# A two-layer pairwise-product network on one core: layer 1 in three rounded passes throughout, five of eight banks to ScalarE in every second tile, GpSimd's program without a loop

## What is computed

```python
for W in filters:                       # x0: 512 x 32 x 32
    z = jnp.einsum('bhd,bmd->bhmd', x0, prev)
    z = z.reshape(b, h * m, d)
    cur = jnp.einsum('bpd,pn->bnd', z, W[0])
    cur = jax.nn.relu(cur)              # 128 maps
    prev = cur
    outs.append(cur)
result = jnp.concatenate(outs, axis=1)
z = jnp.sum(result, axis=-1)            # 512 x 256
...
h = jnp.concatenate([z, dense_ctx], axis=1)
h = jnp.maximum(h @ W_top1 + b_top1, 0.0)
h = jnp.maximum(h @ W_top2 + b_top2, 0.0)
y = h @ W_top3
```

## Time and profile before

| | us |
|---|---|
| median of 3 runs | 882.83 |
| lowest and highest | 880.86, 882.96 |
| profiled execution, its own time | 881.15 |
| its span (first to last instruction) | 879.3 |
| TensorE busy | 854.6 (97%) |
| VectorE busy | 790.5 (90%) |
| ScalarE busy | 681.6 (78%) |
| GpSimd busy | 750.1 (85%) |

### The profile page before, as it was taken

The page is one execution under the profiler, slowest core; times in us unless marked ns, Lnnn a source line. Parts: engine busy times, 40 slices in busy tenths (PEclk is TensorE's granted clock), DMA queues, the critical chain, the costliest instruction groups (busy, mean ns, idle before and its releaser), DMA issues.

```text
span 879.3 us, 18096 instructions
## 1 busy us (share of the span) xinstructions
PE 854.6 (97%) x3581; PEld 669.4 (76%) x3581; DVE 790.5 (90%) x2392; ACT 681.6 (78%) x2230; POOL 750.1 (85%) x834
## 2 busy tenths in 40 slices
PE   2899999999999999999999999999999999999998
PEld 1578777778777777877777787777778777778884
DVE  2689999999999999999999999989999999999984
ACT  2577877888787788888778888777887877888883
POOL 6179989999988999999999999998999989987781
DMA  6786677766667676666777666776766676763430
GB/s 179 205 190 132 157 178 162 181 155 139 126 158 170 163 180 151 136 130 158 173 164 176 142 137 134 164 174 164 167 139 131 144 172 157 182 161 76 88 72 1
DMA packets 55481, 131.16 MB, mean 149 GB/s; under 512 B 8101, under 2 KB 19333, under 8 KB 55462
## 3 DMA queue, kind: packets, MB, share of 16 engines
q0 software_dynamic: 22240, 68.17, 42.8%
q1 hardware_dynamic: 31538, 59.99, 21.2%
q10 hardware_dynamic: 1683, 2.80, 1.0%
HBM read 60.67 MB, written 4.20 MB: 74 GB/s over the span
## 4 chain that ended last, share of the span: by engine, by line
PE 92%; DMA 3%; DVE 2%; SPq 1%; ACT 1%; issue 1%; POOL 0%; DVEq 0%; ACTq 0%
PE t_act L738 13%; PE t_act L740 13%; PE t_act L739 13%; PE t_dve L738 13%; PE t_dve L740 13%; PE t_dve L739 13%; PE acc L706 6%; PE acc L711 5%; DMA x_shift<-x_rows 2%; DMA x_rows<-emb 1%; PE acc_pool L748 1%; PE acc_pool L750 1%; PE acc L715 1%; DVE prod L571 0%; DVE prod L560 0%
## 5 line engine op out<-in xcount | busy, mean ns | idle before, releaser
L412 ACT ACTIVATE prod<-t_act,weigh 128x128 f32<-128x128 f32 x2048 | 577.4, 372 | 117.9 <-PE t_act L740 115.2
L560 DVE SCALAR_TENSOR_TENSOR prod<-t_dve,weigh,prod 128x128 f32<-128x128 f32 x1792 | 482.7, 340 | 11.6 <-PE t_dve L740 6.3
L298 POOL TENSOR_TENSOR prod<-prod 128x512 f32<-128x512 f32 (+1 forms) x255 | 302.3, 1186 | 13.1 <-DMA prod<-prod 2.7
L738 PE MATMUL t_act<-w_hi,cur_hi 128*128 128x512 f32 x512 | 215.8, 422 | 0.1
L738 PE MATMUL t_dve<-w_hi,cur_hi 128*128 128x512 f32 x512 | 199.9, 390 | 3.0 <-DVE prod L560 3.0
L740 PE MATMUL t_act<-w_hi,cur_lo 128*128 128x512 f32 x512 | 200.2, 391 | 0.0
L739 PE MATMUL t_act<-w_lo,cur_hi 128*128 128x512 f32 x512 | 199.9, 390 | 0.0
L740 PE MATMUL t_dve<-w_hi,cur_lo 128*128 128x512 f32 x512 | 199.6, 390 | 0.0
L739 PE MATMUL t_dve<-w_lo,cur_hi 128*128 128x512 f32 x512 | 199.2, 389 | 0.0
L257 POOL DMA_INDIRECT emb<-table_dram,row_ids x128 | 131.7, 1029 | 38.7 <-issue 37.5
L738 PEld LDWEIGHTS t_act<-w_hi,cur_hi 128*128 128x128 f32 x512 | 96.2, 188 | 34.6 <-ACT prod L412 9.0
(11 more groups left out here) (87 smaller groups left out, 624.9 us busy)
## 6 DMA issues: line engine op xcount, KB each, us to landing
prod<-prod POOLq DMA_DIRECT2D x126, 512.0 KB, 5.1
x_shift<-x_rows SPq DMA_DIRECT2D x64, 512.0 KB, 5.6
x_pair<-x_rows SPq DMA_DIRECT2D x96, 128.0 KB
x_same<-x_rows SPq DMA_DIRECT2D x32, 256.0 KB, 4.5
...
emb<-table_dram,row_ids POOLq DMA_INDIRECT x128, 3.6
...
```

What stands on the lines that cost most here:

```text
L298: nc.gpsimd.tensor_tensor(src[:, dst, :], src[:, dst, :], src[:, other, :], ALU.add).then_inc(folded, 1)
L412: last = nc.scalar.activation(prod[i][:, HEADS * k + j, :], t_act[k % ARING][:, j * MAPS:(j + 1) * MAPS], ACT.Copy, scale=weigh[p][:, i, h ...
L560: nc.vector.scalar_tensor_tensor(dst, src, w, dst, ALU.mult, ALU.add).then_inc(added, 1)
L738: nc.tensor.matmul(bank[:, :], cur_hi[p][:, cols], w_hi[:, w], start=True, stop=False)
```

## The change

Five things are done together.

1. In layer 1 groups 0 and 1 also go in three f32r passes. `round_pair` and `lower_pair` are called twice a chunk, once for each pair of groups: groups 2 and 3 of chunk c+1 after tile 0 as before, and groups 0 and 1 of chunk c+2 after tile 3. z_hi and z_lo have four groups in place of two; TensorE tells by `layer1_half` when the first two are free again. Chunk 1's four groups are plain fp32.
2. A table `ORDER` says which engine reads which bank. Tiles 1 and 3 stay ADADADAD. Tiles 0 and 2 are ADAADADA: ScalarE takes five banks, VectorE three, and two t_act banks stand side by side. prod has 20 slots in tiles 0 and 2, the halving adds 10 onto 10, and the fold after it takes three instructions (5, 2 and 1 slots) in place of two (4 and 2).
3. `place` goes from VectorE, after tile 0, to ScalarE, after tile 2, ahead of `relu2`.
4. GpSimd's program is written out for all 32 chunks. `stage` and its `row_ids` are gone, the gathers read `all_ids` at fixed columns and stand ahead of the halving of tiles 0 and 1 in place of behind it; `tick` is gone.
5. After the last chunk, the top layers' first matmuls wait for all of VectorE's additions, where each waited for its own bank. Some small operands lie in freed space.

The diff, cut to its core:

```diff
-HALF = BANKS // 2
-FEEDS = HALF * HEADS
+ORDER = ["ADAADADA", "ADADADAD"] * (TILES // 2)
+A_BANKS, D_BANKS = ([order.count(who) for order in ORDER] for who in "AD")
+A_BEFORE, D_BEFORE = ([sum(banks[:i]) for i in range(TILES + 1)] for banks in (A_BANKS, D_BANKS))
+A_CHUNK, D_CHUNK = A_BEFORE[TILES], D_BEFORE[TILES]
 DRING, ARING = 4, 2
...
-HALVE = (slice(0, 8), slice(8, 16))
-FOLDS = [(slice(0, 4), slice(4, 8)), (slice(0, 2), slice(2, 4))]
+HALVES = [banks * HEADS // 2 for banks in A_BANKS]
+FOLDS = {8: [(slice(0, 4), slice(4, 8)), (slice(0, 2), slice(2, 4))],
+         10: [(slice(0, 5), slice(5, 10)), (slice(0, 2), slice(2, 4)), (slice(0, 1), slice(4, 5))]}
...
-            def stage(c, p):
-
-
-                wait(pool, rows_written[p], before(c, p) * (16 * 2))
-                wait(pool, weigh_ready, c - 1)
-                nc.gpsimd.tensor_copy(row_ids[p][:, :], all_ids[:, bass.ds(c * TILES, TILES)]).then_inc(row_ids_ready, 1)
-
-            def gather(p, which):
-
+            def gather(c, which):
+                p = c % 2
+                if which[0] == 0:
+                    wait(pool, rows_written[p], before(c, p) * (16 * 2))
+                    wait(pool, weigh_ready, c - 1)
                 for i in which:
                     nc.gpsimd.indirect_dma_start(
                         emb[p][:, i * DIM:(i + 1) * DIM], None, table,
-                        bass.IndirectOffsetOnAxis(ap=row_ids[p][:, i:i + 1], axis=0)).then_inc(gathered[p], 16)
+                        bass.IndirectOffsetOnAxis(ap=all_ids[:, c * TILES + i:c * TILES + i + 1], axis=0)
+                        ).then_inc(gathered[p], 16)
...
-            def halve(c, i, staged=None):
-
-                tile = c * TILES + i
-                dst, other = HALVE
-                pool.wait_ge(weighed, (tile + 1) * HALF)
-                pool.wait_ge(added, (tile + 1) * FEEDS)
-                wait(pool, ticked, tile)
-                if staged is not None:
-                    pool.wait_ge(row_ids_ready, staged + 1)
-
-                nc.gpsimd.tensor_tensor(tick[:, :], v[:, 0, 0:TILES], v[:, 1, 0:TILES], ALU.add).then_inc(ticked, 1)
+            def halve(c, i):
+
+                dst, other = slice(0, HALVES[i]), slice(HALVES[i], 2 * HALVES[i])
+                pool.wait_ge(weighed, c * A_CHUNK + A_BEFORE[i + 1])
+                pool.wait_ge(added, (c * D_CHUNK + D_BEFORE[i + 1]) * HEADS)
                 nc.gpsimd.dma_start(prod[i][:, dst, :].rearrange("x h n -> x (h n)"),
                                     prod[i][:, other, :].rearrange("x h n -> x (h n)"),
                                     accum_op=ALU.add).then_inc(halved[i % 2], 16)
...
+                steps = [(slice(0, half), slice(half, 2 * half))] * halve_here + FOLDS[half]
...
-                ahead = not (isinstance(c, int) and c + LEAD >= CHUNKS)
-                first, final = isinstance(c, int) and c == 0, isinstance(c, int) and c == CHUNKS - 1
-                for i in range(TILES - final):
-                    if ahead and i == 0:
-                        stage(c + LEAD, (p + LEAD) % 2)
-                    here = final and i == TILES - 2
+                ahead = c + LEAD < CHUNKS
+                for i in range(TILES - (c == CHUNKS - 1)):
+                    if ahead and i < 2:
+                        gather(c + LEAD, (2 * i, 2 * i + 1))
+                    here = c == CHUNKS - 1 and i == TILES - 2
                     if not here:
-                        halve(c, i, c + LEAD if ahead and i == 0 else None)
-                    if ahead:
-                        gather((p + LEAD) % 2, ((0, 1), (2, 3), (), ())[i])
+                        halve(c, i)
                     if i > 0:
                         fold(c, i - 1, p)
...
-            def round_pair(c, p):
-                act.wait_ge(z_ready, c * 3 + 3)
-                act.wait_ge(layer1_done, c)
-                nc.scalar.activation(z_hi[:, :, :], z[p][:, WHOLE:GROUPS, :], ACT.Copy).then_inc(pair_rounded, 1)
+            def round_pair(c, p, which):
+
+                g = slice(which * 2, which * 2 + 2)
+                act.wait_ge(z_ready, c * 3 + 1 + 2 * which)
+                act.wait_ge((layer1_half, layer1_done)[which], c - 1 + which)
+                nc.scalar.activation(z_hi[:, g, :], z[p][:, g, :], ACT.Copy).then_inc(pair_rounded, 1)
+
+            def place(c, p):
+
+
+                wait(act, pool2_done, c - 1)
+                nc.scalar.copy(sel[p][:, :], sel_wide[:, bass.ds(c * -QUARTERS + (CHUNKS - 1) * QUARTERS, 128)]
+                               ).then_inc(sel_ready, 1)
...
-                for k in range(HALF):
-
-                    act.wait_ge(act_bank, tile * HALF + k + 1)
+                banks = [k for k, who in enumerate(ORDER[i]) if who == "A"]
+                for a, k in enumerate(banks):
+                    n = A_BEFORE[i] + a
+
+                    act.wait_ge(act_bank, c * A_CHUNK + n + 1)
                     for j in range(HEADS):
-                        h = HEADS * 2 * k + j
-                        last = nc.scalar.activation(prod[i][:, HEADS * k + j, :],
-                                                    t_act[k % ARING][:, j * MAPS:(j + 1) * MAPS], ACT.Copy,
+                        h = HEADS * k + j
+                        last = nc.scalar.activation(prod[i][:, HEADS * a + j, :],
+                                                    t_act[n % ARING][:, j * MAPS:(j + 1) * MAPS], ACT.Copy,
                                                     scale=weigh[p][:, i, h:h + 1])
                     last.then_inc(weighed, 1)
...
-                    if i == 0 and not (isinstance(c, int) and c + 1 >= CHUNKS):
-                        round_pair(c + 1, 1 - p)
+                    if i == 0 and not (isinstance(c, int) and (c == 0 or c + 1 >= CHUNKS)):
+                        round_pair(c + 1, 1 - p, 1)
+                    if i == 2:
+                        place(c, p)
+                    if i == 3 and not (isinstance(c, int) and c + 2 >= CHUNKS):
+                        round_pair(c + 2, p, 0)
...
-                if more1:
-                    lower_pair(c + 1, 1 - p)
-                place(c, p)
+                if more1 and not (fixed and c == 0):
+                    lower_pair(c + 1, 1 - p, 1)
...
                     products(c + 2, p, 1)
+                    lower_pair(c + 2, p, 0)
...
-                    if g < WHOLE:
-
-                        if g == 0:
-                            pe.wait_ge(z_ready, c * 3 + 1)
-                        nc.tensor.matmul(acc1[:, :], v[:, g, :], z[p][:, g, :], start=g == 0, stop=False)
+                    if g < GROUPS and isinstance(c, int) and c == 1:
+
+                        pe.wait_ge(z_ready, c * 3 + 1 + 2 * (g // 2))
+                        last = nc.tensor.matmul(acc1[:, :], v[:, g, :], z[p][:, g, :], start=g == 0, stop=False)
+                        if g == WHOLE - 1:
+                            last.then_inc(layer1_half, 1)
                     elif g < GROUPS:
-                        k = g - WHOLE
-                        pe.wait_ge(z_lo_ready, (c - 1) * SPLIT + k + 1)
+                        pe.wait_ge(z_lo_ready, (c - 2) * GROUPS + g + 1)
                         for weights, rows in ((v_hi, z_hi), (v_lo, z_hi), (v_hi, z_lo)):
-                            nc.tensor.matmul(acc1[:, :], weights[:, k, :], rows[:, k, :], start=False, stop=False)
+                            last = nc.tensor.matmul(acc1[:, :], weights[:, g, :], rows[:, g, :],
+                                                    start=g == 0 and rows is z_hi and weights is v_hi, stop=False)
+                        if g == WHOLE - 1:
+                            last.then_inc(layer1_half, 1)
...
-                    n = tile * HALF + k // 2
-                    if k % 2 == 1:
-                        bank, done = t_dve[(k // 2) % DRING], dve_bank
+                    before_k = ORDER[i][:k].count(ORDER[i][k])
+                    if ORDER[i][k] == "D":
+                        n = c * D_CHUNK + D_BEFORE[i] + before_k
+                        bank, done = t_dve[(p * D_CHUNK + D_BEFORE[i] + before_k) % DRING], dve_bank
                         wait(pe, added, (n - DRING + 1) * HEADS)
                     else:
-                        bank, done = t_act[(k // 2) % ARING], act_bank
+                        n = c * A_CHUNK + A_BEFORE[i] + before_k
+                        bank, done = t_act[(A_BEFORE[i] + before_k) % ARING], act_bank
                         wait(pe, weighed, n - ARING + 1)
...
-                pe.wait_ge(added, (CHUNKS * TILES * HALF - DRING + f + 1) * HEADS)
+                pe.wait_ge(added, CHUNKS * D_CHUNK * HEADS)
```

103 lines of the change are left out of this document (47 added, 56 removed).

## The result

| | before | after |
|---|---|---|
| median | 881.85 | 1024.18 |
| lowest and highest | 880.09, 882.96 | 1021.02, 1025.71 |
| profiled execution, its own time | 881.15 | 1023.94 |
| its span | 879.3 | 1022.1 |

The ratio is 1.159, with an interval of 1.154 to 1.163: **slower by 142 us**. The forecast was 926.5, in a range of 905 to 941. The sign is right; 97 us are missing.

A forecast was written before the change was run, and what follows sets the result against it. TensorE's matmuls and its waits were taken to bound each chunk. From 881.15, +42.0 for chunks 1 to 29 and the edges, +45.4 in all, gave 926.5 us; eight-in-ten range 905 to 941.

The forecast's parts named there:

- the last sentence on GpSimd: GpSimd's written-out program needs more instructions fetched; cost bounded by 0 and the 3 to 5 us left at `side`.
- it ends near 22.5 busy us a chunk and is no bound: VectorE in each chunk, after giving up eight multiply-adds and the cast and gaining two z_lo.
- VectorE as the one waited for: A listed sign that the forecast is wrong: waits naming VectorE, where t_act waits behind ScalarE were expected.
- So I take 2.4 GHz throughout: TensorE's clock stays full over the whole run despite four stops a chunk, since the granted clock was 1.000 before.
- The rival with the clock at 1007: TensorE's clock drops to 1.2 GHz for a tenth of the matmuls: +81, 1007 us; chance 0.03.
- The walk of the ring: One chunk walked through the two t_act banks: four TensorE stops in tiles 0, 2 and 3, 1.94 us, period 27.25.
- The term of the sum: Chunks 1 to 29 each pay +1.45 us over the old period of 25.80, 42.0 us together.
- Layer 1: Groups 0 and 1 on TensorE: six f32r matmuls, 1.37 us, replace two fp32, 1.72; 0.35 saved in 30 chunks, 10.5.
- Cost nil: GpSimd: a little less work net, gathers ahead of the halving, 3 to 5 us left before relu2 reads `side`.
- The ring holds: Rival: TensorE gets its banks in time and only layer 1's gain shows, 871.5 us; chance 0.06.
- Only tile 3's stop counts: Rival: the pairs of t_act banks cost nothing by themselves; +0.48 in 30 chunks, 896.5 us; chance 0.10.
- ScalarE's jobs cost more: Rival: the cast takes 0.57, or GpSimd's `side` is late by as much; +0.31 in 31 chunks, 936 us; chance 0.14.

The follow-up runs named there:

- e1: The changed kernel with 32 tiny memsets put into VectorE's stream ahead of its loop, the loop body untouched; 923.58 us.
- e13: The changed kernel with GpSimd's program in a loop again (stage, tick and row_ids as before) and VectorE's loop shifted by 14; 974.75 us.
- e8: The changed kernel with ADADADAD in all four tiles and the selector's cast back on VectorE; 874.29 us, ratio 0.989.

## Why the prediction was wrong in size and right in sign

**The step that failed** is the last sentence on GpSimd: "Written out, the program needs more instructions fetched; no row shows such a cost, bounded by 0 and the same slack." It looked at the engine whose program grew. GpSimd's longest "issue" wait in e1 is 0.3 us, and the queue's traffic grew by four packets (14 in e13, 18 in e1). The cost came on VectorE, whose program shrank: its body slid across an edge and touched four pieces. No term of the sum, and no rival, had a price for an engine's stream that gets shorter ahead of a loop, and "it ends near 22.5 busy us a chunk and is no bound" took VectorE's busy time (22.55, as forecast) for all that it could do to TensorE. "VectorE as the one waited for" stood among the signs of being wrong, and it is what the waits show. It was worth 97.5 us, 2.1 times the whole forecast change. The rule on branches in the section of the Trainium skill named above should have been a rival: before's page has a queue of its own for instructions, with 14 packets, and a loop that jumps back on each engine. Its size could not be had from before's trace, where no body is fetched twice.

**The clock.** "So I take 2.4 GHz throughout" was wrong as a fact, 0.952 in the mean, and right for its reason: the ring's short stops don't lower the clock (e1: 0.996, 1.00 in the window). The rival with the clock at 1007 came out at nearly the measured time, but by another cause. In the loop the clock fell only behind stops of VectorE's making, and it holds about 2.1 of the 7.5 us at the one that was taken apart. At 1.2 GHz matmuls are 0.43 apart there, where the forecast doubled 0.228 to 0.456. The rule of the Trainium skill, "TensorE: Matmul & The Clock Gate", section "A second HAM failure mode: psum-queue depth-cycling", by which short stops at each turn of the banks make the clock oscillate, does not agree with e1.

**The walk of the ring** held, in place and size:

| stop | forecast | measured |
|---|---|---|
| tile 0, bank 3 | 0.36 | 0.30 |
| tile 2, bank 3 | 0.48 | 0.41 |
| tile 3, bank 0 | 0.13 | 0.13 |
| tile 3, bank 4 | 0.97 | 0.82 |
| period | 27.25 | 27.03 |

Half of the difference in the last stop is the cast (0.26 forecast, 0.19 measured); ScalarE's 24.2 busy us are 24.06. The term of the sum was 29 x 1.45 = 42.0 and is 29 x 1.23 = 35.7. What is small there comes back at the edges: between before and e1 the first pooling begins 4.6 later (2.0 forecast, 0.5 for chunk 0 and 1.45 for chunk 1; the forecast names +0.4 for chunk 1's plain fp32 but leaves it out of its sum), chunks 30 and 31 are 0.9 and 1.8 longer (1.0 and 1.4), and what follows them 1.2 (0.5). With the 28 periods between, 28 x 1.235 = 34.6, that adds up to 43.1, the difference of the two spans. That the small and the large sides met so near to 45.4 is luck: the first pooling alone moves by several us from kernel to kernel, as told at e8.

**Layer 1** was right: 1.36 for six matmuls where two took 1.72; e8's 25.36 has no other saving than this and the old stop of 0.14 (0.36 + 0.14 = 0.50, measured 0.44).

**GpSimd**, "Cost nil": right for the program as written, since no window of e1 shows it late. But the argument, a little less work than before, hid that with its loop, `tick` and `stage` kept, GpSimd would have become the bound under the new order (e13, 29.4 a chunk), where in its own stream only the five-slot folds differ from before. The slack of 3 to 5 us at `side` stands only as the new program has it.

**The rivals.** "The ring holds" fell: the pairs stop TensorE. "Only tile 3's stop counts" fell too, since bank 3 of tile 0 and of tile 2 cost 0.71 together. "ScalarE's jobs cost more" fell on the cast, at 0.19 to 0.21.
